# GNN layer on one core: the last edge group gathered between the last scatters and finished beside the variance scan, three groups joined as twelve tiles

## What is computed

```
h       = relu(layernorm(x))                                  # per node
z       = concat(h[src], h[dst], edge_attr)                   # 25000 x 160
e       = sigmoid(z @ W_f + b_f) * softplus(z @ W_s + b_s)    # 25000 x 64
message = segment_sum(e, src, 100000)                         # 100000 x 64
mean, var over the 100000 nodes, per feature
out     = x + h + (message - mean) * rsqrt(var + eps) * gamma + beta
```

## Time and profile before

| | us |
|---|---|
| three timed runs | 1073.52, 1072.77, 1071.25 (median 1072.77) |
| the profiled execution | 1070.97 |
| its span, first to last instruction | 1069.2 |
| stage one, until the first load of the scan | 0 to 865 |
| scan, until the last loads have landed | 865 to 933 |
| variance and output | 934 to 1069 |

### The profile page before, as it was taken

How to read it: one execution, slowest core, us unless ns; L and a number is a source line. 1 busy time by engine, 2 the same in 40 slices (tenths; PEclk the granted TensorE clock), 3 DMA queues, 4 the chain that set the end, 5 groups by cost and what they waited for, 6 DMA issues and landing times. The chain is left out here.

```text
span 1069.2 us, 10789 instructions
## 1 busy us (share of the span) xinstructions
PE 638.0 (60%) x2340; PEld 451.1 (42%) x2340; DVE 734.3 (69%) x1557; ACT 543.7 (51%) x1187; POOL 711.3 (67%) x612
## 2 busy tenths in 40 slices
PE   0436776657755677666576656466666696854332
PEld 0224544445534455444364444344545585620000
DVE  3846886668675767666686656466757638999788
ACT  0425665646655556545466455446454645634232
POOL 7775777877778787777787777887778650040600
PEclk9995665555556555555555565556555659955555
DMA  8997543534544334333344343433333269999999
GB/s 279 416 397 267 128 125 76 124 78 121 124 103 98 86 54 86 87 54 86 54 85 86 55 86 57 82 54 87 53 84 42 20 217 422 379 283 428 414 408 387
DMA packets 87410, 175.63 MB, mean 164 GB/s; under 512 B 41922, under 2 KB 48646, under 8 KB 78928
## 3 DMA queue, kind: packets, MB, share of 16 engines
q1 hardware_dynamic: 34727, 111.07, 28.8%
q0 software_dynamic: 42176, 19.83, 16.4%
q10 hardware_dynamic: 10472, 44.38, 10.2%
HBM read 106.98 MB, written 68.24 MB: 164 GB/s over the span
## 5 line engine op out<-in xcount | busy, mean ns | idle before, releaser
L536 POOL DMA_INDIRECT m_buf<-in_x_dram,m_buf x392 | 376.2, 960 | 120.7 <-issue 112.8
L549 POOL DMA_INDIRECT msgs_dram<-m_buf,target x188 | 295.3, 1571 | 69.4 <-issue 56.4
L1015 PE MATMUL ps_all<-m_buf 128*128 128x64 f32 x940 | 198.2, 402 | 160.1 <-DVE m_buf L756 83.5
L1015 PEld LDWEIGHTS ps_all<-m_buf 128*128 128x128 f32 x940 | 190.6, 311 | 172.0 <-issue 156.1
L648 DVE TENSOR_REDUCE m_buf<-m_last 128x24 f32<-128x1536 f32 x49 | 85.7, 1749 | 52.7 <-ACT m_last L864 52.7
L997 PEld LDWEIGHTS ps_all<-sums,m_buf 128*128 128x128 f32 x392 | 94.7, 331 | 50.6 <-issue 50.6
L912 ACT ACTIVATE m_buf<-m_buf,one_col 128x512 f32<-128x512 f32 x196 | 107.6, 550 | 1.6
L983 PE MATMUL ps_all<-ident,m_buf 128*128 128x128 f32 x196 | 54.3, 432 | 89.4 <-DVE m_buf L716 89.3
L864 ACT ACTIVATE m_last<-m_buf 128x1536 f32<-128x1536 f32 x49 | 72.2, 1473 | 60.0 <-DVE m_buf L619 60.0
L995 PE MATMUL ps_all<-sums,m_buf 128*128 128x512 f32 x98 | 101.7, 1141 | 0.0
L619 DVE SCALAR_TENSOR_TENSOR m_buf<-ps_all,m_buf 128x1024 f32<-128x1024 f32 x98 | 93.9, 958 | 3.9
(11 more groups left out here) (152 smaller groups left out, 994.7 us busy)
## 6 DMA issues: line engine op xcount, KB each, us to landing
m_buf<-msgs_dram SPq DMA_DIRECT2D x38, 1024.0 KB, 17.0
m_buf<-in_x_dram SPq DMA_DIRECT2D x48, 512.0 KB
out_dram<-m_buf ACTq DMA_DIRECT2D x20, 1024.0 KB, 11.3
msgs_dram<-y_kept SPq DMA_DIRECT2D x11, 1536.0 KB
m_buf<-src_rows_dram SPq DMA_DIRECT2D x46, 256.0 KB, 4.0
y_spill_dram<-y_kept ACTq DMA_DIRECT2D x19, 512.0 KB, 4.0
y_kept<-y_spill_dram SPq DMA_DIRECT2D x8, 1024.0 KB, 17.4
msgs_dram<-y_kept ACTq DMA_DIRECT2D x5, 1536.0 KB
```

The costliest lines, as they stand in the source:

```text
L536: pool.indirect_dma_start(xg[:, n % G_SLOTS, 2 * j + c, :], None, x, bass.IndirectOffsetOnAxis(ap=ids[:, c, n * TILES + j:n * TILES + j + ...
L549: pool.indirect_dma_start(msgs, bass.IndirectOffsetOnAxis(ap=target[:, n % UNROLL, j:j + 1], axis=0), comb[:, n % COMB_SLOTS, j, :], None, ...
L1015: pe.matmul(ps_c[:, j, :], same_of(b, j, j + 1)[:, 0, :], msg_of(g)[:, b, :], start=(b == 0 and not joined), stop=(b == j), skip_group_che ...
```

## The change

`LATE` becomes 3: groups 46, 47 and 48 are late, 12 tiles. `PRE` = 48 groups are worked in the steps, and `DRAIN` is 2, so the steps end with 50. Group 48 is gathered apart, by `gather_last`, into memory of its own, and worked on inside the scan's loops by closures that `stage_one` returns to `stage_two` as `last`. The ring of the scan uses 5 buffers (`SCAN_BUFS`) until block 20, because the other three hold group 48's memory; blocks 21, 22 and 23 go to them. The squares use two banks (6 and 2) up to block 17 and three from block 18 on; in blocks 8 to 18 ACT squares 18 rows and PE crosses 14. The memory that `src_all` and `comb` have changes, `S_SLOTS` falls from 3 to 2.

```diff
@@ gpsimd
-        for n in range(GROUPS):
-            if n == LAST:
-                pool.wait_ge(ids_rest, 64)
+        def gather_last(tiles):
+            for j in tiles:
+                for c in range(2):
+                    pool.indirect_dma_start(xg_last[:, 2 * j + c, :], None, x, ...
+                    ).then_inc(last_gathered, 16)
+        for n in range(PRE):
...
+        pool.wait_ge(ids_rest, 64)
         for n in range(behind, EARLY):
+            gather_last([n - behind])
             accumulate(n)
+        gather_last(range(EARLY - behind, TILES))
@@ vector, stage one: after step 49 comes cross_next (masks of group 46 against 47)
-            if g.known and g.back(1).n == LAST:
-                cross_source(g.back(1))
+            if g.known and g.n == STEPS:
+                cross_next()
@@ masks of all three late groups against 48, two of them in memory at a time
+        def mask_last(t):
+            k, b = divmod(t, TILES)
...
+            else:
+                dve.wait_ge(mask_used, t - 1)
+            dve.scalar_tensor_tensor(out=cross_last[t % 2], in0=src_all[:, slot, :, :], ...
+                accum_out=in_last[:, k, b:b + 1]).then_inc(mask_made, 1)
+        def finish():
+            later_ones(g_last)
+            join_later()
+            for k in range(LATE):
+                targets(Group(ITERS, EARLY + k - ITERS * UNROLL))
+            dve.wait_ge(comb_done, GROUPS)
+            dve.tensor_reduce(msg_sum[:, :], ps_sum ...).then_inc(sum_kept, 1)
+        for part in range(TILES):
+            count_not_later(g_last, part)
@@ scalar, end of stage one (it waits for comb_done of group 47)
+        same_source(g_last)
@@ tensor
-            joined = g.known and g.n == LAST
+            joined = g.known and g.n == LAST - 1
+        def join_last(t):
+            pe.wait_ge(mask_made, t + 1)
...
+            for j in range(TILES):
+                ins = pe.matmul(ps_c[:, j, :], cross_last[t % 2][:, j, :], late_msg[:, t, :], ...)
+            ins.then_inc(mask_used, 1)
@@ sync, stage two
         for b, (r0, _) in enumerate(BLOCKS):
             if b == FREE_FIRST:
-                sp.wait_ge(sum_kept, 1)
+                sp.wait_ge(comb_copied, PRE)
+                sp.wait_ge(last_gathered, 16 * GATHERED)
...
+            if b < NB - 1 and before_in_buf(b):
+                sp.wait_ge(rows_squared, chunks_of(before_in_buf(b)[-1]))
+                sp.wait_ge(block_crossed, before_in_buf(b)[-1] + 1)
+            if b < NB - 1 and scan_buf(b) == SCAN_BUFS:
+                sp.wait_ge(msg_done, GROUPS)
+            if b < NB - 1 and scan_buf(b) == SCAN_BUFS + 1:
+                sp.wait_ge(mask_made, (LATE - 1) * TILES)
+            if b < NB - 1 and scan_buf(b) == SCAN_BUFS + 2:
                 sp.wait_ge(comb_copied, GROUPS)
+                sp.wait_ge(corr_done, 1)
@@ scalar, stage two: behind the second piece of a block
+            if k == change:
+                act.wait_ge(banks_blank, 2)
...
+            if r == BANK_ROWS:
+                if b == 5:    last.square()
+                elif b == 6:  last.rstd()
+                elif b == 8:  last.copy_turned()
+                elif b == 10: last.softplus_log()
+                elif b == 11: last.gates()
+                elif b == FINISH_AT: last.copy_comb()        # 17
@@ tensor, stage two: behind a block's crossing; two banks are cleared first, five later
+            if b == 7:    last.turn()
+            elif b == 8:  last.products()
+            elif b == 9:  last.join(0)
+            elif 11 <= b < 16: last.join(b - 10)
+            elif b == 16: last.join(6); last.join(7); last.combine()
+            elif b == FINISH_AT:
+                pe.wait_ge(sum_kept, 1)
+                pe.wait_ge(comb_copied, GROUPS)
+                for bank in sorted(set(range(PSUM_BANKS - 1)) - set(SQ_FIRST)):
+                    ins = clear(bank)
+                ins.then_inc(banks_blank, 1)
@@ vector, stage two: begins with a wait for group 47; behind a block's last piece
+        dve.wait_ge(comb_done, PRE)
...
+            if b == 0:    list_spare()
+            elif b == 4:  last.centre()
+            elif b == 5:  last.sum_squares()
+            elif b == 6:  last.normalise()
+            elif b == 8:  last.mask(0)
+            elif b == 10: last.mask(1); last.softplus()
+            elif b == 11: last.message(); last.mask(2)
+            elif 12 <= b < 15: last.mask(b - 9)
+            elif b == 15: last.mask(6); last.mask(7)
+            elif b == FINISH_AT: last.finish(); take_means(); mark_nodes()
+            elif b == CORRECT_AT: correct()                   # 18
+            elif b == LIST_AT: list_targets()                 # 19
-            if k + 1 == chunks_of(b) and order[0] + 1 <= b < order[0] + 1 + BETA_PARTS:
-                take_mean(b - order[0] - 1)
+            if order[0] + 2 <= b < order[0] + 2 + BETA_PARTS:
+                take_mean(b - order[0] - 2)
```

More of the change, by code:

```diff
@@ L77 @@
 M_BUFS = 8
+SCAN_BUFS = 5
 FREE_FIRST = 3
 SQ_ROWS = 20
-SQ_BANKS = (5, 6, 4)
+SQ_BESIDE = 18
+BESIDE = range(8, 19)
+SQ_FIRST = (6, 2)
+SQ_THEN = (6, 4, 5)
+SQ_CHANGE = 18
 Y_ROWS = 32
@@ L479, in load @@
         def load(g):
-            if g.back(S_SLOTS).exists() and not (g.known and g.n < 2 * S_SLOTS):
+            if g.back(S_SLOTS).exists() and not (g.known and g.n < UNROLL):
                 load_sources(g.back(S_SLOTS))
@@ L513, in sync @@
                 load(Group(0, u))
+        for u in range(S_SLOTS, UNROLL - S_SLOTS):
+            load_sources(Group(0, u))
         with sp.Fori(1, ITERS) as it:
@@ L516, in sync @@
                 load(Group(it, u))
-        for u in range(GROUPS - LAST + S_SLOTS):
-            load(Group(ITERS, u))
+        load(Group(ITERS, 0))
+        load_edges(g_last)
+        load(Group(ITERS, 1))
+        load_sources(g_last)
     def gpsimd(pool):
@@ L768, in step @@
                 later_ones(g.back(3))
-                if g.known and g.back(3).n == LAST:
-                    later_in_last()
-                    targets(g.back(4))
-                if not (g.known and g.back(3).n == LAST - 1):
+                if not g.back(3).late:
                     targets(g.back(3))
@@ L1034, in tensor, with turn_last @@
         run_groups(pe, step, DRAIN)
+        def turn_last():
+            pe.wait_ge(h_done, EDGES_TURN)
+            pe.wait_ge(z_copied, PRE)
+            for j in range(TILES):
+                ins = pe.transpose(ps_z[:, j, :], xc_last[:, 2 * j:2 * j + 2, :].rearrange("p c f -> p (c f)"),
+                                   ident[:, :])
+            ins.then_inc(z_turned, 1)
+            turn_edges(g_last)
+        def join_last(t):
+            pe.wait_ge(mask_made, t + 1)
+            if t == 0:
+                pe.wait_ge(comb_copied, PRE)
+            for j in range(TILES):
+                ins = pe.matmul(ps_c[:, j, :], cross_last[t % 2][:, j, :], late_msg[:, t, :],
+                                start=(t == 0), stop=False, skip_group_check=True)
+            ins.then_inc(mask_used, 1)
+        last = Shared()
+        last.turn = turn_last
+        last.products = lambda: products(g_last)
+        last.join = join_last
+        last.combine = lambda: combine(g_last)
+        return last
     return Programs(sync, gpsimd, vector, scalar, tensor)
@@ L1159, in wait_m @@
             b = buf_of(i)
-            loads = len([k for k in range(NB - 1) if k % M_BUFS == b]) + len(
+            loads = len([k for k in range(NB - 1) if scan_buf(k) == b]) + len(
                 [k for k in in_ring[M_BUFS:] if k <= i and buf_of(k) == b])
@@ L1331, in tensor @@
             ins.then_inc(block_crossed, 1)
+            if b == 7:
+                last.turn()
+            elif b == 8:
+                last.products()
+            elif b == 9:
+                last.join(0)
+            elif 11 <= b < 16:
+                last.join(b - 10)
+            elif b == 16:
+                last.join(6)
+                last.join(7)
+                last.combine()
+            elif b == FINISH_AT:
+                pe.wait_ge(sum_kept, 1)
[3 more added lines that the diff above has]
+                ins.then_inc(banks_blank, 1)
             if Y_BLOCK < b <= Y_BLOCK + Y_FIRST:
@@ L1422, in correct, with mark_nodes @@
                               ).then_inc(corr_done, 1)
[L1424 to L1428 removed]
+        def mark_nodes():
             for k in range(LATE):
```

399 lines of the change are left out of this document (267 added, 132 removed).

## The result

| | before | after |
|---|---|---|
| timed runs, median | 1073.01 us (20) | 1074.82 us (20) |
| ratio | | 1.0021 [1.0014, 1.0028] |
| profiled execution (its span) | 1070.97 (1069.2) | 1073.69 (1071.9) |
| first loads of the scan | 865.18 | 848.09 |
| VectorE's first add | 874.05 | 863.55 |

The 20 runs of each kernel include one that took twice as long, which the ratio leaves out. The kernel is 0.2% slower: the direction forecast, at a sixth of the size (+1.8 us by the medians, where 1084 stood for +11).

A forecast was written before the change was run, and what follows sets the result against it. GpSimd bounds stage one, DMA and VectorE the scan, DMA the output. Scan end -12.1 + 14.1 + 0.5 + 8 = +10.5, plus 0.8 for patches, on 1070.97 gives 1082.3, median 1.8 higher: 1084 us (1077 to 1091; wider range 1069 to 1096).

The forecast's parts named there:

- first add: Start of the scan: VectorE's first addition of squares at about 865.2 instead of 874.05, 8.9 us earlier.
- the seam: Between stage one and scan: first loads near 848, 17 us earlier, of which 8.9 are left for VectorE.
- `combine(47)` at the lower price: TensorE ahead of the scan: combining group 47 takes 12.4 us, its 52 products at 1.2 GHz, 0.22 us each.
- The rival that had it at the upper level: TensorE from 846 on at the upper clock: 52 products in 6.6 us, not 11.6; total 1074; chance 0.10.
- gaps for data: Start of the scan: VectorE's waits for blocks 3, 5, 6 and 7 go, 3.2 us less.
- work of the last group and `correct`: VectorE in the scan: centring, masks, softplus, message, `finish`, sums and a longer `correct` add 14.1 us.
- adds: VectorE's additions of squares in the scan: 0.5 us more for two banks; 2 rows fewer save nothing net.
- stalls: VectorE's waits in the scan for ScalarE, TensorE and bank clearing: 8 us more, bounds 0 and 20.
- PE stays behind: Scan blocks with a mask multiplication for the last group: 2.9 us for TensorE against 2.65 for VectorE.
- the 2 us that mask 7 was to wait for it: Scan: VectorE's mask 7 of the last group waits 2 us for TensorE's join 5, the mask-by-message multiplication.
- the gaps absorb it: Rival, scan: the 14.1 us fill VectorE's 9.6 idle us; scan ends 4.6 earlier, total about 1070; chance 0.10.
- the short seam: Rival, start of the scan: loads streaming from 848 decide, scan ends 17 us earlier, total 1060; chance 0.05.

The follow-up runs named there:

- no_correct: Changed kernel without three of the four operations of `correct` (2.9 us of VectorE); 1070.96 us, 0.9995 of the kernel before.
- join_twice: Changed kernel with each of the last group's eight mask-by-message multiplications done twice, on a slower chip; 1099.82 us, 1.0137 of the kernel before.
- after_acts: Changed kernel with ScalarE's softplus logarithm and `copy_comb` moved behind the third square of blocks 10 and 17, slower chip; 1090.05 us, 1.0050 of the kernel before.
- spread_change: Changed kernel with group 48's same-source sums spread over scan blocks, three banks and copies of y from block 19; 1070.75 us, 1.0001 of the kernel before.
- all_moved: Changed kernel with the edits of both spread_change and after_acts, on the slower chip; 1086.39 us, 1.0009 of the kernel before.
- sq20: Changed kernel with ScalarE squaring 20 rows instead of 18 in blocks 8 to 18; 1075.18 us, 1.0043 of the kernel before.
- before_2banks: Kernel before with its squares in two banks instead of three, nothing else changed; 1072.84 us, 1.0021 of the kernel before.
- before_again: Kernel before, unchanged, run again for a trace in the fourth batch; 1071.33 us, ratio 0.9993.
- after_third: Changed kernel, unchanged, third sample, in the fourth batch; 1074.61 us, 1.0025 of the kernel before.
- all_moved2: Changed kernel with the edits of all_moved, repeated in the fourth batch where the kernel before takes 1072; 1069.82 us, 0.9975 of the kernel before.
- after_again: Changed kernel, unchanged, run once more in the first batch; 1074.14 us, 1.0025 of the kernel before.

## Why the prediction was wrong in size

**Right.** The direction, the mechanism, and the seam. First loads near 848: 848.09. Loads from block 3 on at 859.3: 859.23. `combine(47)` at the lower price: the row at 846.14 has 7.06 for 32 products, the row of before 7.09. The rival that had it at the upper level is out, though its 1074 is the number closest to the 1074.8 measured: that it fits is luck. Its granted clock (windows with the columns of the earlier trace rows):

```profile
845.00:855.00 10.00, 8.86 (x42) 8.89 (x42) 2.65 (x14) 2.85 (x10) 7.79 (x8) 0.50 0.72 236
855.00:865.00 10.00, 9.56 (x40) 8.04 (x40) 2.06 (x5) 5.86 (x16) 7.55 (x8) 0.50 0.80 290
```

The trace disagrees with what I took from the Trainium skill (TensorE: Matmul & The Clock Gate, Part 1), that sustained matmul activity releases the clock: these 52 products, one behind the other for 11 us, ran at 0.50. The gaps for data went. GpSimd's period of 17.5 us did not change, and a later scan end moves the end of the kernel one for one (no_correct).

**Wrong.** The step is the sum at the end of the scan, +10.5, where +1.9 was measured; four of its terms were mis-sized, and all to the same side (first pair of traces):

| term | forecast | measured | off |
|---|---|---|---|
| first add | -8.9 | -10.5 | -1.6 |
| gaps for data | -3.2 | -3.2 | 0 |
| work of the last group and `correct` | +14.1 | +13.6 | -0.5 |
| adds | +0.5 | -3.2 | -3.7 |
| stalls | +8 | +5.2 | -2.8 |
| sum | +10.5 | +1.9 | -8.6 |

- *Stalls.* I priced TensorE's block with a join at 1.9 + 1.0 = 2.9 from the lengths of grouped rows. Such a length holds the tail of the last instruction, beside which the next group already runs. From start to start 14 products are 1.62 (895.92 to 897.54) and a join 0.83 (895.09 to 895.92). TensorE's block is 2.45, not 2.9, and VectorE's 2.46, not 2.65. So "PE stays behind", 0.25 us in each block with a join, and the 2 us that mask 7 was to wait for it were false: no gap stands at block 15. These 2 us are most of the 2.8. join_twice shows how near it was: with 0.9 us more a block the stalls I had forecast appear. The waits at blocks 10 (1.48), 17 (2.66) and 18 (1.06) were all in the sum, and after_acts, spread_change and all_moved show that they are ScalarE's order and the clearing of banks: with all of these moved 1.25 us of waits are left of 5.20.
- *Adds.* I charged 0.5 for the third bank and let the 2 rows fewer cancel. Measured: the three adds of a block that has other work behind it take 1.79 (896.18 to 897.97). In the kernel before a block without other work takes 2.11 (908.48 to 910.59), and one with other work 1.91:

```profile
919.44 2.00 DVE L1460 TENSOR_TENSOR sums<-sums,ps_all 128x512 f32<-128x512 f32 x3
921.35 0.69 DVE L1406 TENSOR_TENSOR m_buf<-m_buf,sums 128x512 f32<-128x512 f32 x1
```

  So 0.20 a block goes as soon as another operation stands between the blocks, and the rest is the rows: they did not cancel but saved 1.6 in all (sq20), while two banks cost 1.0 and not 0.5 (before_2banks). That the extra operation gives ScalarE time to be ahead with the next square, so that the short pauses between adds go, is my reading. This is a part of the rival "the gaps absorb it", which had a tenth: of the 3.2 us by which the adds got shorter 1.6 are the rows, so about 1.6 of the 13.6 were absorbed.
- *First add.* The two DMA issues (0.9) cost nothing, at 860.70 beside ScalarE's activations, and `combine(47)` began 0.4 us earlier than I had shifted it (846.14 for 846.5); the last 0.3 are small differences behind it.

The sign "DVE busy over 55 of the 60 us" was missed as well: from 863.55 on it is 49.6, no more than before. The work did not make VectorE busier, it made the scan longer. The room in a block was smaller than I said, 0.4 and not 0.5 us, since an undisturbed block costs 2.11 and not 2.0, and the short seam would have had 69 us for VectorE's work, not 67; neither changes a term of the sum.

The sizes are those of one pair of traces. In the second pair (before_again, after_third) the last reduce is 3.9 later and not 1.9: the first add is again 10.5 earlier, the work again 13.6 and the stalls 5.1, but the kernel before had only 0.9 us of waits for data to lose. By the medians the three pairs give +1.8, +2.9 and +2.7 us.

Behind the scan +0.8 was forecast and +0.8 measured (+0.4 in the second pair), though the reload came 19.3 behind the variance and not 17.5; what they are stays open.

The changed kernel's gain was therefore real, 10.5 + 3.2 at the seam, and was given back as 13.6 of VectorE's work in a scan where VectorE waited 3.2 us for data (0.9 in the second trace of the kernel before), and 5.2 of stalls. Order alone, the same-source sums out of the seam and the stalls' causes moved, gave 4.8 us back by the medians, which makes the difference between 1.0025 and 0.9975.

**Left open.** Why on the slower chip the same edits gave 1.0050 and 1.0009. There the seam is longer: the first three loads start at 857.53 and the next at 876.17 (in after_acts), 18.6 us apart and not 11; TensorE waits there for VectorE's masks of step 48, which come 14.8 us later than in the changed kernel's first trace while GpSimd's gathers are 5.2 later. There is no trace of the kernel before on that chip.

## What to carry to other kernels

Price a loop that two engines share by the distance from start to start of its instructions, not by the length of a grouped row: at 14 and 8 instructions the difference was 0.4 us a block, and it decided which engine waits. When work of an earlier stage goes beside a later one that is bound by something else, count first what the engine that is to take it has to spare, here 0.9 to 3.2 us of VectorE's waits and about 1.6 in short pauses, then what the moved work needs ahead of the later stage, and put each producer behind the instruction that this engine waits for next, not ahead of it. A seam gained by an early load is worth only what the first consumer can use of it: of 17.1 us, 10.5.

## What was not expected of the hardware

TensorE's granted clock fell in the scan behind some short pauses, and in the two cases shown (below and in all_moved2) VectorE's wait that came of it was longer than the pause. In the kernel before with two banks TensorE waited 1.82 us for ScalarE at 906.77; its windows (columns as in the earlier trace rows):

```profile
895.00:905.00 10.00, 6.42 (x48) 5.66 (x48) 8.61 (x15) 4.86 (x11) 0.00 (x0) 1.00 1.02 424
905.00:915.00 10.00, 8.23 (x28) 5.78 (x28) 8.37 (x14) 8.64 (x18) 0.00 (x0) 0.65 1.01 416
915.00:925.00 10.00, 10.00 (x31) 6.54 (x31) 6.69 (x12) 4.55 (x9) 0.00 (x0) 0.50 1.01 422
925.00:935.00 10.00, 10.00 (x91) 10.00 (x91) 9.29 (x15) 5.29 (x11) 3.33 (x2) 1.00 0.71 263
```

It ran at 0.50 (the lower level, 1.2 GHz) for 17 us, without a pause, the 12 products of a crossing at 2.93 instead of 1.60; VectorE came to wait 2.52 for it. In all_moved2 the pause was 2.06 and the lower level lasted 13.5 us. In the changed kernel three pauses (2.36, 2.75 and 2.21 us) were followed by 3 to 4 us at the lower level, and one of 1.97 by none. The length of the pause alone doesn't decide it: in after_third one of 3.11 was followed by none, in after_again one of 2.86. So a kernel whose TensorE is near the edge can lose time to one wait of a neighbour, and not in every execution.

A 128x768 element-wise operation on GpSimd took 1.5 to 1.8 us, and three of VectorE's operations beside it became up to eight times longer (0.23 to 1.88). Each of them ended within 0.1 us of GpSimd's operation, while VectorE's adds from PSUM beside the fourth one kept their 1.87 us, and its reduce from PSUM its 0.41.

The chips differ by more than the change: the kernel before took 1071 to 1073 us as the median of four sets of runs and 1085 in a fifth, on another chip.
